# A macaron block with strided attention on one core: a folded prologue in another order, and a guard on the exponents that reads only the weights

## What is computed

```python
x = x + 0.5 * ffn(layernorm(x))        # first FFN
x = x + attention(layernorm(x))        # 16 heads of 8, key j allowed if j % 4 == 0 or |i - j| <= 8
x = x + 0.5 * ffn(layernorm(x))        # second FFN, same weights
# ffn: h = x @ W_exp + b_exp (128 -> 512); h = butterfly(h, up_weights); h = gelu(h + up_bias)
#      h = butterfly(h, down_weights); y = h @ W_con + b_con + down_bias
# butterfly: 9 stages, stage s mixes the pairs (i, i ^ 2**s) with a 2x2 matrix of its own
# attention: q *= sigmoid(unity_scale); scores / sqrt(8); softmax; @ v; @ o_w + o_b
```

## Time and profile before

| | |
|---|---|
| median of 3 runs (lowest, highest) | 269.37 us (268.79, 269.70) |
| the profiled execution, its time | 269.3 us |
| its span, first to last instruction | 267.5 us |
| TensorE busy | 249.6 us, 93% of the span |
| ACT / DVE / POOL busy | 196.4 (73%) / 126.7 (47%) / 7.3 us (3%) |
| moved by DMA | 21.82 MB, mean 82 GB/s |

### The profile page before, as it was taken

How to read it: one execution, slowest core, us unless ns; L and a number is a source line. 1 busy time by engine, 2 the same in 40 slices (tenths; PEclk the granted TensorE clock), 3 DMA queues, 4 the chain that set the end, 5 groups by cost and what they waited for, 6 DMA issues and landing times.

```text
span 267.5 us, 6937 instructions
## 1 busy us (share of the span) xinstructions
PE 249.6 (93%) x2919; PEld 138.3 (52%) x2919; DVE 126.7 (47%) x408; ACT 196.4 (73%) x256; POOL 7.3 (3%) x12
## 2 busy tenths in 40 slices
PE   1698899999789999999999999999999999899995
PEld 0482766857434344445444445434455444457775
DVE  4878357898776232035254135134235422446113
ACT  1764165576779999998899988999978999654440
POOL 9100000000000000000000000000000000000000
PEclk9999999999999999999999999999999999999999
DMA  6940000187669743411311330331230000000112
GB/s 201 269 122 9 2 1 0 56 254 208 169 169 352 245 89 80 85 57 34 87 54 32 86 84 4 87 83 36 53 86 2 0 4 2 2 0 0 42 39 78
DMA packets 23887, 21.82 MB, mean 82 GB/s; under 512 B 4743, under 2 KB 22087, under 8 KB 23835
## 3 DMA queue, kind: packets, MB, share of 16 engines
q1 hardware_dynamic: 22742, 21.02, 29.1%
q10 hardware_dynamic: 1112, 0.34, 0.6%
HBM read 13.98 MB, written 7.56 MB: 81 GB/s over the span
## 4 chain that ended last, share of the span: by engine, by line
PE 87%; ACT 5%; DVE 4%; DMA 1%; issue 1%; DVEq 0%; ACTq 0%
PE ps L670 23%; PE ps L648 22%; PE ps L494 11%; PE ps L450 9%; PE ps L655 4%; PE ps L680 4%; PE ps L464 2%; PE ps L688 2%; PE ps L700 1%; PE ps L476 1%; PE ps L437 1%; PE ps L530 1%; DMA resid<-L_attn_x 1%; PE ps L517 1%; PE ps L516 1%
## 5 line engine op out<-in xcount | busy, mean ns | idle before, releaser
L868 ACT ACTIVATE probs_all<-ps 128x1024 f32<-128x1024 f32 x128 | 122.8, 1023 | 11.1 <-PE ps L648 9.4
L670 PE MATMUL ps<-probs_all,v_strided 128*32 128x256 f32 x1024 | 68.2, 384 | 0.2 <-ACT probs_all L868 0.2
L648 PE MATMUL ps<-q_slots,k_strided 75*128 75x512 bf16 x250 | 65.3, 381 | 0.3 <-ACT probs_all L868 0.3
L670 PEld LDWEIGHTS ps<-probs_all,v_strided 128*32 128x32 f32 x1024 | 27.2, 109 | 31.8 <-issue 9.5
L1146 DVE RECIPROCAL rden<-ps 128x16 f32<-128x16 f32 x16 | 4.1, 258 | 72.1 <-PE ps L688 72.1
L648 PEld LDWEIGHTS ps<-q_slots,k_strided 75*128 75x128 bf16 x250 | 20.4, 97 | 33.6 <-issue 9.8
L450 PE MATMUL ps<-xnorm_t,up_folded 128*128 128x512 f32 x64 | 29.3, 601 | 1.7 <-ACT xnorm_t L757 1.0
L494 PE MATMUL ps<-down_folded,gelu_h 128*128 128x128 f32 x192 | 22.7, 277 | 1.2 <-ACT gelu_h L766 1.2
L766 ACT ACTIVATE gelu_h<-ps,bias_up 128x512 f32<-128x512 f32 x24 | 16.4, 687 | 10.0 <-PE ps L450 9.9
L494 PEld LDWEIGHTS ps<-down_folded,gelu_h 128*128 128x128 f32 x192 | 22.0, 192 | 2.9 <-issue 2.1
L1172 DVE SCALAR_TENSOR_TENSOR probs_all<-probs_all,mask_k_sb 128x1024 f32<-128x1024 f32 x16 | 19.6, 1223 | 3.0 <-ACT probs_all L874 2.5
(11 more groups left out here) (119 smaller groups left out, 227.5 us busy)
## 6 DMA issues: line engine op xcount, KB each, us to landing
q_slots<-q_parts SPq DMA_DIRECT2D x16, 288.0 KB
k_local<-k_local_parts SPq DMA_DIRECT2D x48, 78.0 KB
q_parts<-prologue_or_parts SPq DMA_DIRECT2D x9, 384.0 KB, 4.5
k_strided<-k_strided_parts SPq DMA_DIRECT2D x12, 96.0 KB
q_parts<-last_parts SPq DMA_DIRECT2D x3, 384.0 KB, 4.7
k_local_parts<-prologue_or_parts SPq DMA_DIRECT2D x3, 288.0 KB, 4.8
resid<-L_attn_x SPq DMA_DIRECT2D x1, 768.0 KB, 10.0
out<-resid SPq DMA_DIRECT2D x3, 256.0 KB, 2.3
```

The source lines that it names most:

```text
L648: mm = pe.matmul(PS[:, b0 + i, :], KS[:, ch, G * g + h, :], QS[:, g, h, :], start=True, stop=True)
L670: mm = pe.matmul(PS[VC * h:VC * (h + 1), 6 + n % 2, 0:QB // 2], VS[:, ch, at:at + VC], probs, start=(ch == 0 and r == 0), stop=False, skip ...
L868: act.activation(PE_[:, ch // 2, 2 * m:2 * m + 2, ch % 2, :], PS[:, b0:b0 + 2, :], ACT.Exp).then_inc(p_ready, 1)
```

## The change

Three parts.

**Prologue.** Only six of the nine stages are folded into one factor on either side (a 128x512 matrix each); the last two up stages and the first down stage are applied to the products instead, by DVE. Up: TensorE multiplies W_exp by the factor in four matmuls of 128 columns, then DVE does stage seven (a product 1,024 wide, a sum 512 wide), stage eight (product 1,024, two sums of 256 that write UPW directly). Down: ACT scales 8 blocks of W_con, DVE sums 512, multiplies 1,024, sums 512, and TensorE finishes with four matmuls of 128 columns, now behind up(0). One DMA brings all far rows and one a selector (8 KB and 512 B a row) in place of four DMAs. The near weights shrink from 516 KB to 260 KB each. The load order on SP is x block 0, up, W_exp, down, W_con, rest of x; W_exp leaves ACT's queue and the unity scale goes from its last place to its third. ACT first waits for that scale, does the exponential and loads the GELU table, and only then normalizes block 0. POOL's two large memsets wait for block 0's layer norm. Matmuls that nobody reads (`keep_warm`, on W_exp) stand at three places. DVE normalizes block 2 right behind block 1.

**Order.** The rows of block 0 are turned behind down(1), not before it. The last block's values are computed behind score step 2 of the first unit, and ACT copies them out between the second and third exponential; six early scores and two `keep_clock` matmuls go. On SP the key loads of groups 2 and 3 stand behind the write of block 2's strided keys.

**Guard.** From q_w (scaled) and k_w alone: the Gram matrix of each head (`gram`), masked by head (DVE, `BG`), its square (`gram_squared`), its fourth power (`gram_fourth`), whose squared entries summed bound the eighth power of the largest eigenvalue; `traces` sums by head, DVE multiplies and compares, `count_kept` counts. SAFE goes from 40 to 68. Squares, sums by head and maxima of the data go.

```diff
-UPN = NC * (2 ** STAGES // NC * 2 - 2)
+UPN = NC * (2 ** STAGES // NC - 2)
...
-SAFE = 40.0
+SAFE = 68.0
...
             sp.dma_start(X[:, 0:TB, :], x_t[:, 0:TB, :]).then_inc(ld_x[0], 16)
+            sp.dma_start(WUP[:, :], up_near).then_inc(ld_up, 16)
+            sp.dma_start(WT[:, :, :], w_exp_t.rearrange("(c p) d -> p c d", p=P)).then_inc(ld_wt, 16)
             sp.dma_start(WDN[:, :], dn_w).then_inc(ld_dn, 16)
-            sp.dma_start(WUP[:, :], up_near).then_inc(ld_up, 16)
             sp.dma_start(WCON[:, :, :], w_con.rearrange("(c p) d -> p c d", p=P)).then_inc(ld_wc, 16)
...
                 sp.wait_ge(kl_out[c], 16)
-            for g in range(NG):
+            for g in range(2):
                 load_k(0, g, ld_q[g])
             write_strided(2)
+            for g in range(2, NG):
+                load_k(0, g, ld_q[g])
             write_strided(NB - 1)
...
+            pool.wait_ge(xb_ready, 1)
...
                 for c in chunks:
+                    if b == 0:
+                        pe.wait_ge(upw_sb, c // 2 + 1)
+                    if b == 0 and c == 2:
+                        pe.wait_ge(bup_set, 1)
...
-            pe.wait_ge(one_set, 1)
-            pe.wait_ge(ld_uf, 16 * NC)
+            def keep_warm(bank, n):
...
+            def spread(r, i):
...
+            pe.wait_ge(ld_uf, 16 * 2)
             for r in range(NC):
+                spread(r, 0)
+            spread(0, 1).then_inc(six_bc, 1)
+            for r in range(1, NC):
+                spread(r, 1).then_inc(wbc, 1)
+            pe.wait_ge(ld_wt, 16)
+            keep_warm(1, 1)
+            pe.wait_ge(up_fold, STAGES - 3)
+            for c in range(NC):
+                mm = pe.matmul(PS[:, 1, c * P:(c + 1) * P], WT[:, c, :], UPB[STAGES - 3][:, c * P:(c + 1) * P], start=True, stop=True)
+            mm.then_inc(upw_ps, 1)
             pe.wait_ge(ld_id, 16)
             transpose_block(0)
...
+            pe.wait_ge(sev_sb, 1)
+            keep_warm(6, 2)
             ffn_up(0)
+            pe.wait_ge(dn_fold, STAGES - 3)
+            pe.wait_ge(wc_mix, 1)
+            for j in range(NC):
+                mm = pe.matmul(PS[:, 7, j * P:(j + 1) * P], DNB[-1][:, j * P:(j + 1) * P], CONS[:, j * P:(j + 1) * P], start=True, stop=True)
+            mm.then_inc(dnw_ps, 1)
...
                     if last and t == 2:
+                        if b < NB:
+                            count_kept()
                         pe.wait_ge(y_done, b)
...
                     ffn_up(b)
                     if b < NB - 1:
                         transpose_block(b + 1)
+                if b == 2:
+                    skip_hint = pe.mark_branch_hint_location()
                 if b == NB:
-                    skip_hint = pe.mark_branch_hint_location()
-                    norm_sums(NB - 2)
                     pe.wait_ge(y_first, 1)
                     keep_clock(0, 1)
-                if b:
+                    pe.wait_ge(flag_set, 1)
+                    bounded = pe.value_load(FLAG[0:1, 0:1], min_val=0, max_val=1)
+                if b > 1:
                     turn_rows(b - 1)
+                if b == NB - 1:
+                    traces()
                 if b < NB:
                     ffn_down(b)
-                if 2 <= b < NB:
-                    norm_sums(b - 2)
                 if b == 0:
+                    keep_warm(7, 1)
                     transpose_block(1)
+                if b == 1:
+                    turn_rows(0)
+                if b == 1:
+                    gram()
+                if b == 2:
+                    gram_fourth()
                 if b:
                     keys_queries(b - 1)
                 if 0 < b < NB:
                     block_values(b - 1, 0, None)
...
+                if b == 1:
+                    gram_squared()
+            pe.br_cond(bounded == 0, "pe_large_bound", "pe_bounded").branch_hint(skip_hint)
...
-                            scores(it, g, s)
+                        if it == 0 and g == 0 and s < 2:
+                            pe.wait_ge(qk_ready, 3 * NB - 1 + s)
+                        scores(it, g, s)
+                        if it == 0 and g == 0 and s == 2:
+                            block_values(NB - 1, 0, None)
+                        if it == 0 and g == 0 and s == 3:
+                            pe.wait_ge(v_ready, 3 * NB)
                         if before and s == 1:
...
+            act.dma_start(FAR[0:P:32, :, :], up_far).then_inc(ld_uf, 16)
+            act.dma_start(SEL[0:P:32, :, :], far_sel).then_inc(ld_uf, 16)
+            act.dma_start(UN[:, :], unity[None, :].partition_broadcast(P).rearrange("p a b -> p (a b)")).then_inc(ld_un, 16)
...
             act.wait_ge(ld_un, 16)
...
+            act.wait_ge(xb_ready, 1)
+            for t in range(TB):
+                act.activation(XN[:, 0, t, :], X[:, t, :], ACT.Identity, bias=XB[:, t:t + 1], scale=RS[:, t:t + 1]).then_inc(xn_ready, 1)
+            act.wait_ge(wbc, 3)
+            act.activation(SEVENS, PS[:, 6:8, :].rearrange("p a b -> p (a b)"), ACT.Copy).then_inc(sev_sb, 1)
+            act.wait_ge(ld_dn, 16)
+            act.wait_ge(ld_wc, 16)
+            for h in range(2):
+                for m in range(NC):
+                    n = h * NC + m
+                    ins = act.activation(CON8[:, n * P:(n + 1) * P], WCON[:, 2 * h + m // 2, :], ACT.Copy, scale=WDN[:, n:n + 1])
+            ins.then_inc(wc_far, 1)
             operand(0)
-            act.wait_ge(upw_ps, 1)
-            act.activation(UPW[:, :], PS[:, 1, :], ACT.Copy).then_inc(upw_sb, 1)
             for b in range(NB + 1):
                 if b < NB:
                     gelu(b)
+                if b == 0:
+                    act.wait_ge(dnw_ps, 1)
...
                 if b >= 1:
+                    if b == 1:
+                        act.activation(BQ[:, :], QW[:, :], ACT.Copy, scale=SG[:, 2:3]).then_inc(bq_ready, 1)
+                    if b == 2:
+                        act.wait_ge(bd_ps, 2)
...
                     qkv(b - 1)
+                    if b == 2:
+                        act.wait_ge(bd_ps, 3)
+                        act.activation(BG4[:, :, :].rearrange("p a k -> p (a k)"), PS[:, 7, 0:2 * P], ACT.Square).then_inc(bd_act, 1)
...
+                        if u == 0 and s == 2:
+                            values_out(NB - 1)
...
             dve.wait_ge(ld_up, 16)
             mix(KUP, WUP, up_mix)
-            for st in range(1, STAGES - 2):
+            for st in range(1, STAGES - 3):
...
+            dve.wait_ge(six_bc, 1)
+            widen(UPB[STAGES - 3], UPB[STAGES - 4], PS[:, 3, :].rearrange("p (m h s) -> p m h s", m=NC, h=2), NC, up_fold)
...
+            dve.wait_ge(ld_dn, 16)
+            for st in range(1, STAGES - 3):
+                pairwise(DNB[st], DNB[st - 1], WDN[:, at:at + n], dn_fold)
+            dve.wait_ge(wbc, 3)
+            pairwise(DNB[STAGES - 3], DNB[STAGES - 4], PS[:, 2, :], dn_fold)
+            dve.wait_ge(upw_ps, 1)
+            dve.wait_ge(sev_sb, 1)
+            widen(UP7, PS[:, 1, :], SEVENS.rearrange("p (m h s) -> p m h s", m=NC, h=2), NC, fold_step)
+            dve.tensor_tensor(UP7S.rearrange("p (a s) -> p a s", a=2), u7[:, :, 0], u7[:, :, 1], ALU.add).then_inc(fold_step, 1)
+            widen(UP8, UP7S, PS[:, 4:6, :].rearrange("p a (h s) -> p a h s", h=2), 2, fold_step)
+                dve.tensor_tensor(UPW[:, c], UP8[:, 0:HID][:, c], UP8[:, HID:2 * HID][:, c], ALU.add).then_inc(upw_sb, 1)
...
+            dve.wait_ge(wc_far, 1)
+            dve.tensor_tensor(CON4, CON8[:, 0:HID], CON8[:, HID:2 * HID], ALU.add).then_inc(fold_step, 1)
+            dve.tensor_tensor(CONM.rearrange("p (m k d) -> p m k d", m=NC, k=2),
+            dve.tensor_tensor(CONS, CONM[:, 0:HID], CONM[:, HID:2 * HID], ALU.add).then_inc(wc_mix, 1)
             dve.wait_ge(ld_x[1], 16)
             layernorm(TB, NT - TB)
             dve.wait_ge(xn_ready, TB)
             normalize(1, XN, xn_ready)
+            dve.wait_ge(xt_ps, 1)
+            normalize(2, XN, xn_ready)
...
+                if last and b < NB:
+                    bound_product()
                 if last:
                     dve.wait_ge(y_half, b // NB + 1)
                     sum_tiles(b, 0, 2, y_first)
                     if b < NB:
                         dve.wait_ge(y_first, 1)
                         statistics(b * TB, 2)
+                        bound_flag()
                 dve.wait_ge(y_ps, b + 1)
                 sum_tiles(b, 2 if last else 0, TB, y_done)
...
-                if b < NB - 2:
-                    ffn_ahead(b + 1)
+                if b == 1:
+                    ffn_ahead(2)
                 if b == NB - 1:
                     split_part(NB - 2, 0)
-                if b >= 2:
-                    norms(b - 2)
+                if b == 1:
+                    dve.wait_ge(bd_ps, 1)
+                    dve.tensor_tensor(BG[:, :, :].rearrange("p a k -> p (a k)"), PS[:, 7, 0:2 * P], BM[:, :, :].rearrange("p a k -> p (a k)"),
```

(5 more changed lines are left out.)

262 lines of the change are left out of this document (115 added, 147 removed).

## The result

The changed kernel takes 268.57 us (median of 19 runs, 266.28 to 275.70), the kernel before 269.43 beside it (19 runs). The ratio is 0.995, with a 95% interval of 0.9930 to 0.9971: faster, by 0.9 us or 0.3 to 0.7%. The profiled execution took 268.35 us with a span of 266.4. I forecast 265.0, with 267.8 as the upper end: of 4.3 us only about one came. The median lies on the bound that I gave for "faster", 268.6.

A forecast was written before the change was run, and what follows sets the result against it. TensorE, 87% of the chain that ended last, was taken to bound the kernel. Keys at 69.4 plus 12.7 put unit 1 at 82.1 against 86.43, so 269.3 - 4.3 = 265.0 us, range 263.0 to 267.8.

The forecast's parts named there:

- The likeliest case: Whole kernel: unit 1 at 82.1 against 86.43, time 265.0 us; chance 0.56, own range 264.2 to 266.0.
- K: The keys at the end of block 3, from which the attention entry is counted: 69.4 against 71.44.
- Memsets: Prologue: L916 no longer waits for POOL's memset (1.64 to 0.17); memsets beside DVE's two-input products cost nothing.
- The two new DMAs are the first of their queue and I start them at 4.7.: Prologue: TensorE starts spreading the eight far rows at 4.7, against 5.38 before.
- The unity scale at 6: Prologue, ScalarE: the scale's transfer, issued third at 1.6, lands at 6; up to 7.9 it costs nothing.
- The rival: Prologue: the unity scale lands late, at 9.5, and everything behind it is 1.6 later, 266.6 us; chance 0.12.
- Low clock through up(0): Rival, prologue: TensorE's low clock lasts through up(0), which takes 3.6 more; 271 us, slower; chance 0.07.
- VectorE's folding and block 1's operand: Prologue, down side: folding ends at 19.7, block 1's operand is ready at 26.1, up(1) at 27.0 against 31.94.
- TensorE stalls 2.0 us, and its squares cost 0.45.: End of block 1: `gram_squared` waits for DVE's `grams` until 41.6; up(2) at 42.1 against 44.21.
- `traces` 1.0: Block 3, ahead of down(3): `traces` waits for DVE's reduction at 59.7 and costs 1.0; down(3) at 59.8.
- K = D3 + 9.6, unit 1 = K + 12.7: Block 3's end and attention entry: 8.2 + 1.4 from down(3) to the keys, then 12.7 to unit 1 at 82.1.
- the change's largest cost: End of block 1: the 2.0 us wait for `grams`, with up(2) and all of block 2 queued behind it.

The follow-up runs named there:

- e6: e2's kernel without the dummy product of 512 columns ahead of the four narrow up products: 265.79 us.
- e4: The changed kernel with ScalarE normalizing block 0 and copying stage seven's weights before it waits for the unity scale: 268.24 us.
- e2: The changed kernel with the Gram squares moved from the end of block 1 behind block 1's rows in block 2: 264.35 us.
- e11: The changed kernel with the edits of e2, e4 and e5, without the two dummy products ahead of up(0): 265.39 us, against 263.10 with them.
- e1: The changed kernel with two dummy products of 512 columns in front of TensorE's wait for the Gram matrices: 266.81 us.
- e5: e2's kernel with `traces` in the middle of block 3's down product, `count_kept` behind it and two small VectorE steps later: 263.64 us.
- e3: The changed kernel without the guard's computation, its flag set by a memset and the branch kept: 262.25 us.
- e8: e2's kernel with the unity scale's transfer issued first on ScalarE's queue, ahead of the far rows' two transfers: 266.52 us.

## Why the prediction was wrong, point by point

The likeliest case had the mechanism right in every part but one, and the sum ended 3.2 us short at unit 1. On the profile's scale, forecast and measured:

| point | forecast | measured | late by | new there |
|---|---|---|---|---|
| first far product | 4.7 | 5.70 | 1.0 | 1.0 |
| up(0) | 16.0 | 17.19 | 1.2 | 0.2 |
| up(1) | 27.0 | 28.27 | 1.3 | 0.1 |
| up(2) | 42.1 | 43.98 | 1.9 | 0.6 |
| up(3) | 54.2 | 57.08 | 2.9 | 1.0 |
| down(3) | 59.8 | 63.03 | 3.2 | 0.3 |
| K | 69.4 | 72.66 | 3.3 | 0.1 |
| unit 1 | 82.1 | 85.33 | 3.2 | 0 |

**Memsets.** Right: 0.17 for 1.64, and 4.13 us of memset beside VectorE's two-input products cost them nothing.

**"The two new DMAs are the first of their queue and I start them at 4.7."** Wrong by 1.0. The kernel before had its four far rows at 5.38; two transfers in their place came at 5.70, and in none of the twelve other traces before 5.11. The issue of the first, into every 32nd partition, took 1.12 us by itself. From there to up(0) I counted 11.3, and it was 11.5. As forecast, the dummy and not VectorE's factor held the narrow product back (11.29; without the dummy it starts at 10.25 in e6). What came on top was the late copy.

**The unity scale at 6.** It came at 9.05, past the 7.9 that I gave as harmless and near my bound of 9.5. The rival priced a landing at 9.5 at 1.6; this one cost 0.5 at the most, as e4 and the row of e2 show.

**Low clock through up(0).** It did not come (3.67). The clock had risen before the two dummies; e11 shows that without them it falls again ahead of up(0), for 1.7 and not the 3.6 that I had priced for a clock that stays low.

**VectorE's folding and block 1's operand.** Up(0) to up(1) is 11.08, forecast 11.0. Right.

**"TensorE stalls 2.0 us, and its squares cost 0.45."** The stall was 2.12, ended by the instruction I named. But what a stall does to the clock I left out. I had used the lower clock only for the beginning of the program, where the earlier trace rows show it, and treated it as gone once it had risen. The squares took 0.93 for 0.45, and up(2) 1.27 more (e1, e2). **This is the failed step**: its 1.75 us are over half of the 3.2 that are missing, and it is the only mechanism that was absent from the sum. Without them the profiled 268.35 would be 266.6 by my estimate, inside the range that I gave. The late first product (1.0), the late copy (0.2 at up(0)) and the stall's own 0.1 make nearly all the rest. By the Trainium skill's page "TensorE: Matmul & The Clock Gate", Part 1, the section on oscillation, waits of TensorE put it back to the throttled state, so that the next stretch starts slow. The trace agrees (0.72 behind the stall), though the waits in that section's example are of 3 to 5 us and this one was 2.12; I had weighed Part 1 only for how the clock comes up.

**`traces` 1.0.** It waited 1.58. VectorE did as forecast: down(3) starts 9.4 us behind the sum of block 2, as I had it. The wait is longer because TensorE was there sooner: up(3) to the end of the rows took 4.1 where I allowed 4.6, so this costs down(3) nothing. What the wait was worth is what I had priced: 1.05 by e5. The 1.3 us that the table shows as new at up(3) and down(3) are up(2)'s fall in clock, which reached VectorE's sum as well (53.60, forecast 50.4). Behind this wait the clock did not fall: the down product has its usual durations.

**K = D3 + 9.6, unit 1 = K + 12.7.** Measured 9.63 and 12.67. The strided keys ended no wait.

Why did so much disappear? The prologue's gain was real (5.2 at up(0)), and the guard took it back: 6.6 us by e3's distance, of which my sum had 2.0 + 0.45 + 0.45 + 1.0 and some tenths, 4, as "the change's largest cost". The place matters more than the amount of work: 5.2 of these 6.6 us go when two calls are moved behind work that is ready.

## What to carry to other kernels

Put a small product whose input another engine still computes behind the next block's work on TensorE, not ahead of it; here one such call cost 4.2 us for 0.45 of work. A TensorE stall is to be priced with what follows at the lower clock, and where it can't be moved, two dummy products in it are worth more than silence (1.8 us by e1's trace, not clear of noise in its times; 1.7 by e11's, and clear there). And compare traces from the landing of the first transfer on, since that moved by 1.3 us between executions with no edit to it, more than several of the effects looked for.

## What the runs showed of the hardware

- **The clock can fall in a short stall.** After 2.12 and 2.11 us idle (the change, e4) and 2.07 (e11) the granted clock behind was 0.70 to 0.76 and eight 512-column products took 4.90, 5.22 and 5.37 us for 3.70. After 1.57 and 1.58 us it stayed at full speed. It does not fall each time: two of the change's 19 executions had a mean clock of 1.000 and were 2 us faster than its median. But a mean clock of 1.000 is no sure sign of a short time either: in e4 three of the four such took 268.11 to 268.35, and the profiled one, at 0.994, took 267.59.
- **The granted clock in the records does not show the slow start.** It reads 1.00 from 11 to 12.5 us in the change, where the narrow product's first five records take 421 ns, and stays at 1.00 behind, where the transposes take 272. When the durations change differs between executions: the same eight records took 1.51, 1.62 or 1.91 us.
- **The issue of one DMA can be dear.** 1.12 us for 16 KB into four partitions that lie 32 apart, where its neighbours took 0.44 to 0.56. The pattern alone is not it: the selector's 4 KB into the same four partitions took 0.51.
- **A tiny broadcast can hold up others** (e8): placed first, 0.5 KB cost the whole kernel 2.2 us.
